# A gated delta-rule layer: the four steps of a block decayed at once, their carries by stored products, and a new order around them

## The reference

```python
def step(S, xs):
    q_t, k_t, v_t, a_t, b_t = xs
    Sk = jnp.einsum('bhvk,bhk->bhv', S, k_t)
    S = a_t[..., None] * S - (b_t[..., None] * (Sk - v_t))[..., None] * k_t[:, :, None, :]
    o_t = jnp.einsum('bhvk,bhk->bhv', S, q_t)
    return (S, o_t)
```

## Time and profile before

| | |
|---|---|
| median of 3 runs | 2696.94 us (2694.35 to 2698.34) |
| profiled execution | 2697.37 us, its span 2695.6 us |
| mean granted TensorE clock | 0.889 |
| busy | PE 2205.7 us, DVE 1928.7, ACT 1279.0, POOL 555.7 |
| transfers | 434.41 MB in 211139 packets |

### The profile page before, as it was taken

One profiled execution on the slowest core, in us unless ns is written; L12 is line 12 of the kernel. 1 busy time (PEld: TensorE's weight loads), 2 busy tenths in 40 slices (PEclk: granted clock), 3 DMA queues, 4 the chain that ended last, 5 costly groups with the idle time before them and its releaser, 6 DMA issues.

```text
span 2695.6 us, 61331 instructions
## 1 busy us (share of the span) xinstructions
PE 2205.7 (82%) x21482; PEld 1634.8 (61%) x21482; DVE 1928.7 (72%) x4376; ACT 1279.0 (47%) x2731; POOL 555.7 (21%) x580
## 2 busy tenths in 40 slices
PE   5999999999937778777877777787787773599998
PEld 3445888888736667666766666666676662244443
DVE  5222899999928878888887888888888788133334
ACT  2000787778715445444544544554454450334433
POOL 0000343444432212212222222122122222000000
PEclk9999999999958888788887888978888895799999
DMA  6000477667775455555555554554555554301210
GB/s 235 8 8 13 161 270 273 236 234 275 275 255 181 155 194 172 180 167 179 178 170 179 171 193 151 184 189 155 186 180 157 192 172 140 137 5 73 78 62 24
DMA packets 211139, 434.41 MB, mean 161 GB/s; under 512 B 47152, under 2 KB 160552, under 8 KB 181720
## 3 DMA queue, kind: packets, MB, share of 16 engines
q1 hardware_dynamic: 210856, 430.95, 46.8%
q0 software_dynamic: 48, 0.16, 0.0%
HBM read 295.13 MB, written 136.98 MB: 160 GB/s over the span
## 4 chain that ended last, share of the span: by engine, by line
PE 49%; DVE 23%; issue 13%; ACT 12%; DMA 1%; DVEq 1%; POOL 1%; ACTq 0%; SPq 0%; POOLq 0%
PE PS L1342 11%; DVE arena L945 8%; ACT arena L740 5%; PE PS L1454 4%; PE PS L1481 4%; PE PS L1330 4%; PE PS L1294 3%; PE PS L1244 3%; PE PS L1221 3%; DVE arena L972 2%; DVE arena L1000 2%; ACT arena L745 2%; PE PS L1467 2%; PE PS L1476 2%; PE PS L1356 2%
## 5 line engine op out<-in xcount | busy, mean ns | idle before, releaser
L1244 PE MATMUL PS<-arena 128*128 x2048 | 463.6, 387 | 1.8 <-DVEq L930 0.9
L945 DVE SCALAR_TENSOR_TENSOR arena<-PS,SM,arena 128x256 f32<-128x256 f32 x1152 | 452.8, 474 | 15.5 <-ACT arena L650 15.5
L1244 PEld LDWEIGHTS PS<-arena 128*128 128x128 f32 x2048 | 383.8, 188 | 81.6 <-DVE arena L945 6.5
L1342 PE MATMUL PS<-arena 128*128 128x128 f32 x1920 | 340.0, 331 | 84.5 <-ACT arena L745 84.5
L1342 PEld LDWEIGHTS PS<-arena 128*128 128x128 f32 x1920 | 286.9, 229 | 126.4 <-ACT arena L745 101.7
L577 POOL TENSOR_TENSOR arena<-arena 128x256 f32<-128x256 f32 x128 | 114.6, 896 | 1188.6 <-DVE arena L1044 1188.6
L740 ACT ACTIVATE arena<-arena 128x128 f32<-128x128 f32 x960 | 302.0, 394 | 32.9 <-DVE arena L989 32.3
L650 ACT ACTIVATE arena<-PS,SM 128x256 f32<-128x256 f32 x384 | 209.5, 564 | 89.3 <-PE PS L1244 84.3
L766 ACT COPY arena<-PS 128x512 f32<-128x512 f32 (+1 forms) x188 | 91.1, 521 | 304.6 <-PE PS L1369 304.2
L1330 PE MATMUL PS<-ident,arena 128*128 128x128 f32 x960 | 184.9, 326 | 61.0 <-ACT arena L740 60.2
L754 ACT COPY arena<-PS 128x256 f32<-128x256 f32 x240 | 89.5, 373 | 257.7 <-PE PS L1342 256.7
(11 more groups left out here) (134 smaller groups left out, 3558.2 us busy)
## 6 DMA issues: line engine op xcount, KB each, us to landing
arena<-g_d SPq DMA_DIRECT2D x128, 1024.0 KB, 5.1
arena<-vas_d SPq DMA_DIRECT2D x128, 384.0 KB, 3.2
vas_d<-arena SPq DMA_DIRECT2D x32, 1024.0 KB, 10.1
kq_d<-arena SPq DMA_DIRECT2D x8, 4096.0 KB, 11.5
arena<-kq_d SPq DMA_DIRECT2D x16, 2048.0 KB, 8.2
arena<-beta_d SPq DMA_DIRECT2D x8, 2048.0 KB, 9.1
kb_d<-arena SPq DMA_DIRECT2D x8, 2048.0 KB, 10.3
vas_d<-arena SPq DMA_DIRECT2D x8, 2048.0 KB, 12.5
```

Source lines behind the costliest of these rows:

```text
L945: nc.vector.scalar_tensor_tensor(acc, raw[:, :, i:i + PT_], CW[:, w, i, hh:hh + 1], acc, ALU.mult, ALU.add).then_inc(job_free if i == TAPS ...
L1244: ins = mm(dst.rearrange("p (b n) -> p b n", b=B), W4[:, w, kt, DH * h:DH * (h + 1)], XNT[:, kt, :, bass.ds(c * PT_ + (HALO - halo), halo ...
L1342: ins = mm(bank(7)[:, 128 * gi:128 * (gi + 1)].rearrange("v (l x) -> v l x", l=NB), STR[:, s % 2, gi, :], KQ[d][:, :, p0:p0 + 2].rearrange ...
```

## The change

Each block decays all its reads at once by products from the block's start (`dec`), adds all values at once (`add`), and decays a write to the later steps of the block (`carry`) before it is weighed. The products needed (1, a1, a1*a2, a2, a0, a0*a1, a0*a1*a2: `ND_` = 7 a step group) are made by GpSimd in the projection (`steps`, a quarter of the heads at a time, in a tile for one quarter), stored to `t_d` and loaded with GB. `NACC` falls from 6 to 3. In the order of the chunk loop: VectorE adds state slots right behind a block's copy for blocks 0 to 4; TensorE issues g4 ahead of g0 in blocks 1 and 3; ScalarE copies g0 there after its read copies. In `carry(1)` the factors 0:4:3 are 1 and a2.

```diff
-NACC = 6
+NACC = 3
+ND_ = 7
+    t_d = dram("t_d", (128, NS * NB, ND_ * NP))
+        TSTf = take(PSC * NB * ND_ * NP // 4)
+        DT = take(2 * ND_ * NP).rearrange("v (b p x) -> v b p x", b=2, x=ND_)
+        DW = take(3 * NP).rearrange("v (p x) -> v p x", x=3)
...
+                def store_steps(q):
+                    w = ND_ * NP // 4
+                    sp.wait_ge(t_step, c * 20 + 5 * q + 6)
+                    sp.dma_start(t_d[:, blocks, w * q:w * (q + 1)], TSTf.rearrange("v (l x) -> v l x", x=w)).then_inc(t_stored, 16)
+                store_steps(0)
                 store_decays(0)
                 sp.wait_ge(silu_done, c * NQ + NACC + 2 * NQ // 3)
                 sp.dma_start(kq_d[two].rearrange("s k x -> k s x"), ...).then_inc(kq_stored, 16)
+                store_steps(1)
                 sp.wait_ge(kb_step, c * 8 + 8)
                 sp.dma_start(kb_d[two].rearrange("s k x -> k s x"), ...).then_inc(kb_stored, 16)
                 store_suffixes(0)
+                store_steps(2)
                 store_decays(1)
+                store_steps(3)
...
+                sp.dma_start(DT[:, m % 2].rearrange("v p x -> v (p x)"), t_d[:, at(n * NB + m)].rearrange("v l x -> v (l x)")).then_inc(t_in[m % 2], 16)
...
+                def steps(q):
+                    a, k = AQ[:, q], c * 20 + 5 * q + 1
+                    pool.wait_ge(a_ready, c * 4 + q + 1)
+                    pool.wait_ge(t_stored, c * 64 + 16 * q + 64)
+                    if q == 0:
+                        pool.wait_ge(t_step, k)
+                    tt(TS[..., 5], a[..., 0], a[..., 1], ALU.mult).then_inc(t_step, 1)
+                    tt(TS[..., 2], a[..., 1], a[..., 2], ALU.mult).then_inc(t_step, 1)
+                    nc.gpsimd.tensor_copy(TS[..., 1:4:2], a[..., 1:3]).then_inc(t_step, 1)
+                    nc.gpsimd.tensor_copy(TS[..., 4], a[..., 0]).then_inc(t_step, 1)
+                    pool.wait_ge(t_step, k + 4)
+                    tt(TS[..., 6], TS[..., 5], a[..., 2], ALU.mult).then_inc(t_step, 1)
...
                         if x == NQ // 3:
+                            steps(0)
                             pool.wait_ge(beta_in, c * 16 + 16)
...
                     if x == 6:
+                        steps(1)
                         suffixes(0)
+                steps(2)
+                steps(3)
                 suffixes(1)
...
                         act.wait_ge(sf_stored[i // 4], c * 16 + 16)
+                        act.wait_ge(t_stored, c * 64 + 32 * (i // 4) + 32)
...
-                        if k > 0:
+                        if k > 0 and m not in (1, 3):
                             next_evac()
...
-                    def add(t):
-                        tt(W[:, :, t], V[:, :, t], W[:, :, t], ALU.add).then_inc(v_add, 1)
-                    def dec(t):
-                        xs = Xb[:, :, :, t + 1:4]
-                        tt(xs, xs, A[:, :, t].unsqueeze(2).unsqueeze(3).to_broadcast([128, NP, 2, 3 - t]), ALU.mult).then_inc(x_dec, 1)
+                    def dec():
+                        dve.wait_ge(corr_sub, n * N_SUB + (9 if m == 0 else SUB_AT[m - 1] + 1))
+                        dve.wait_ge(t_in[m % 2], n * 64 + (16 * (m // 2) + 16))
+                        xs = Xb[:, :, :, 1:4]
+                        tt(xs, xs, wide(D[:, :, 4:7], 0), ALU.mult).then_inc(x_dec, 1)
+                    def add():
+                        dve.wait_ge(x_dec, n * NB + m + 1)
+                        tt(W, V, W, ALU.add).then_inc(v_add, 1)
+                    def carry(t):
+                        ...
+                        tt(DW[:, :, t:3], W[:, :, t].unsqueeze(2).to_broadcast([128, NP, 3 - t]), f, ALU.mult).then_inc(w_dec, 1)
...
-                    dec(0)
+                    dec()
+                    add()
+                    carry(0)
                     weigh(0)
-                    add(1)
-                    sub(0)
...
+                    sub(0)
+                    carry(1)
                     weigh(1)
-                    dec(1)
-                    add(2)
-                    sub(1)
...
+                    sub(1)
                     weigh(2)
-                    dec(2)
-                    add(3)
...
-                    if m == 3 and nxt:
-                        state_add(6)
-                        state_add(7)
+                    if nxt and m < 5:
+                        state_add(2 * m if m < 4 else 10)
+                        state_add(2 * m + 1 if m < 4 else 11)
...
-                    if bk == 0:
+                    if bk == 0 or what == "g4":
                         pe.wait_ge(corr_sub, ...)
...
+                    if m == 1 or m == 3:
+                        preps.reverse()
```

More of the change, by code:

```diff
@@ L262, in build @@
         e_stored, half_bias = sem("e_stored"), sem("half_bias")
+        t_step, t_stored, t_in, w_dec = sem("t_step"), sem("t_stored"), [sem(f"t_in{i}") for i in range(2)], sem("w_dec")
         kq_in = [sem(f"kq_in{i}") for i in range(2)]
@@ L340, in _ @@
                 sp.sem_inc(stored, 16)
+            sp.sem_inc(t_stored, 64)
             sp.wait_ge(xnT_ready, 8)
@@ L419, in _ @@
                 sp.wait_ge(stored, 16 * NPC + 16)
+            sp.wait_ge(t_stored, 64 * NPC + 64)
             sp.wait_ge(job_full, NPC * NJ)
@@ L519, in _ @@
             ES = EST.rearrange("v (s r p) -> v s r p", s=PSC, r=7)
-            with pool.Fori(0, NPC) as c:
+            TS = TSTf.rearrange("v (l p x) -> v l p x", p=NP // 4, x=ND_)
+            AQ = ASTf.rearrange("v (l q p t) -> v q l p t", q=4, p=NP // 4, t=BL)
+            for stored in base_stored:
+                pool.wait_ge(stored, 16 * NX // 2 + 16)
+            pool.wait_ge(beta_stored, 16 * B)
+            nc.gpsimd.memset(TS[..., 0], 1.0).then_inc(t_step, 1)
+            with pool.Fori(0, NPC) as c:
+                def steps(q):
[10 more added lines that the diff above has]
+                    tt(TS[..., 6], TS[..., 5], a[..., 2], ALU.mult).then_inc(t_step, 1)
                 def suffixes(hf):
@@ L562, in _ @@
                 pool.wait_ge(stored, 16 * NPC + 16)
+            pool.wait_ge(t_stored, 64 * NPC + 64)
             for tile in (S, PT32, KBT):
@@ L696, in _ @@
                 act.wait_ge(stored, 16 * NPC + 16)
+            act.wait_ge(t_stored, 64 * NPC + 64)
             act.wait_ge(zeros, 5)
@@ L969, in head_sub @@
                     dve.wait_ge(corr_full, n * 9 + 1 + hf)
-                    if b == 0:
-                        dve.wait_ge(v_add, n * NB * BL + 1)
+                    if b == 0 and hf == 0:
+                        dve.wait_ge(x_read, 1 + n * 16)
                     tt(dst, dst, src, ALU.subtract).then_inc(corr_sub, 1)
@@ L980, in level_sub @@
                     dve.wait_ge(nested, n * 7 + NEST_BEFORE[m])
-                    if k == 0:
-                        dve.wait_ge(v_add, (n * NB + m + 1) * BL + 1)
                     tt(dst, dst, src, ALU.subtract).then_inc(corr_sub, 1)
@@ L1033, in weigh @@
                             dve.wait_ge(gb_in[m % 2], n * 64 + (16 * (m // 2) + 16))
-                            dve.wait_ge(v_add, k4 + 1)
-                        else:
-                            dve.wait_ge(x_sub, k3 + t)
-                        tt(TMP[:, :, 0:6 - 2 * t].rearrange("v p (e t) -> v p e t", e=2), GB[:, m % 2, :, t, :, t + 1:4],
-                           W[:, :, t].unsqueeze(2).unsqueeze(3).to_broadcast([128, NP, 2, 3 - t]), ALU.mult).then_inc(wg_mul, 1)
+                        if t < 2:
+                            dve.wait_ge(w_dec, (n * NB + m) * 2 + t + 1)
+                            w = DW[:, :, t:3]
+                        else:
+                            dve.wait_ge(x_sub, k3 + 2)
+                            w = W[:, :, 2:3]
+                        tt(TMP[:, :, 0:6 - 2 * t].rearrange("v p (e t) -> v p e t", e=2), GB[:, m % 2, :, t, :, t + 1:4], wide(w, t), ALU.mult).then_inc(wg_mul, 1)
                     def sub(t):
                         dve.wait_ge(wg_mul, k3 + t + 1)
-                        dve.wait_ge(v_add, k4 + t + 2)
                         xs = Xb[:, :, :, t + 1:4]
@@ L1046, in chunk @@
                     Pt, at = {4: (P4, 0), 8: (P8, 4), 16: (P16, 12), 32: (P32, 28)}[LEVEL[m]]
-                    add(0)
                     if m == 0:
@@ L1111, in chunk @@
                         for s in ADD_AT[m]:
-                            if m != 3 or s >= 8:
+                            if m >= 5 or m == 3 and s >= 8:
                                 state_add(s)
```

19 lines of the change are left out of this document (8 added, 11 removed).

## The result

The changed kernel takes 2681.6 us (median of 5 runs, 2679.7 to 2683.5), the kernel before, run beside it, 2694.6 (5 runs, 2694.1 to 2698.3). The ratio is 0.9948, interval [0.9934, 0.9963]: 14 us faster by the ratio, where 24 were forecast. The profiled execution has a span of 2681.2 us against 2695.6, 14.4 less. That difference is split here.

A forecast was written before the change was run, and what follows sets the result against it. It took VectorE to bound the projection and no engine alone the chunk loop. Loop -40, projection +7 and tail +9 gave -24 from 2697.4: 2673 us, own range 2655 to 2690, 80% range 2630 to 2715.

The forecast's parts named there:

- The chunk loop, -40: Chunk loop: 2.65 us off a chunk as a mean, fifteen times, with small terms for last and first chunk; net 40 us off.
- the mask wait: Block 1 to 2: VectorE's 3.53 us idle for the g4 mask moves to the corrections and is no gain of that size.
- TensorE's clock moves: Rival, chunk loop: granted clock rises from 0.83 to 0.86, 19 us more off, twice that at 0.89; chance 0.18 for up.
- Block 0 to 1: Chunk loop: ScalarE's and TensorE's waits go; 1.6 us off in one chunk of a pair, 0.5 in the other.
- Block 1 to 2: Chunk loop: TensorE's wait for ScalarE's scaling falls, 1.2 us off a chunk.
- The block arithmetic, 0.15 to 0.42 us a block: Chunk loop: VectorE 0.4 us less busy a block; 0.15 us counts from corrections to copy, 0.4 at block 3 to 4.
- The projection, +7: Projection: the suffix store lands 3 to 5 us later, VectorE stalls 1.0 us an iteration, seven times: 7 us.
- the tail, +9: End of the projection: the last e store, which GpSimd's memsets wait for, lands 9 us later (6 to 14).
- GpSimd and its stores take turns: Rival, projection: calls of 4.9 us or packets of 33 ns lengthen the round round one tile; 2703 us, chance 0.14.
- the beta load 9 us later: Projection: the beta load moves back about 9 us, costing GpSimd 6 us, taken up by the wait for the kq transfer.
- the upper bound 38: Projection: by bytes alone a 448-byte packet costs 38 ns, a store 4.9 us, transfers 61.5 us an iteration, over the period.
- a doubling, 52 ns: Rival, projection stores: each 448-byte packet handled as a read and a write, 6.7 us a store; 2755 us, chance 0.08.

The follow-up runs named there:

- e3: The changed kernel with the old order of the chunk loop (products, stores and loads stay); 2724.0 us, ratio 1.0109.
- e4: The changed kernel with step products made by GpSimd in the chunk loop, two blocks ahead, none made or stored in the projection, NACC 6; 2644.8 us, ratio 0.9814.
- e2: The kernel before with the state additions alone moved right behind the copy, g4 and g0 as before; 2644.7 us, ratio 0.9815.
- e7: The changed kernel with two quarter tiles in turn for the step products and NACC 2; 2663.4 us, ratio 0.9877.
- e6: The changed kernel without GpSimd's step products in the projection, a tile of ones stored four times an iteration instead; 2661.3 us, ratio 0.9871.
- e5: The changed kernel with step products made but not stored, the chunk loop loading other data in their place; 2646.6 us, ratio 0.9819.
- e8: The changed kernel with one tile for half the heads, stored twice an iteration in 896-byte packets, NACC 2; 2684.2 us, ratio 0.9960.
- e12: The kernel before with g4 alone issued ahead of g0 in blocks 1 and 3, additions where they were; 2695.4 us, ratio 1.0002.

## Why the prediction was right, and where it was not

The direction and the range were right, the size was 14 instead of 24. That it came so near has luck in it: the loop gave 8 us more than forecast and the projection cost 19 more (35 for 16), and the loop's gain came by another way than the sum has it.

**The chunk loop, -40: measured -47.7.** The waits that the prediction named went, the mask wait went over to the corrections as it said, and it put no gain there. The sum had 2.65 us off each chunk; what happened is that 13 of 14 chunks became shorter by one step of some 3.5 us (95.6 to 92.1). With the clock's part taken out by the rough estimate above, 40 us are left; that this is the term itself is chance. The clock rose too, as in the rival "TensorE's clock moves": from 0.83 to 0.85 in the window of the earlier trace rows (0.86 was priced). Half of its matmul time was taken to be on the chain; the estimate has 0.4.

**The split of the 40 was wrong.** "Block 0 to 1" was given 1.6 and 0.5 us, 16 us in fifteen chunks: alone it gave 40 (24 without the clock, by the estimate). "Block 1 to 2" was given 1.2 us, 18 us: it gave 6.5. So a wait that the trace names as the last need not be worth its length. The two lengths of a chunk say how this can be: the additions moved in block 0 bring 13 chunks down by a step, those in block 1 three. Why a step is as long as it is, and how much of it is waits and how much clock, stays open; no run held the clock still.

**The block arithmetic, 0.15 to 0.42 us a block.** The busy saving came: in e3 VectorE is busy for 1151.2 us between the first and last `carried` instead of 1202.6, over 120 blocks 0.43 us a block, where 0.4 was taken. (The forecast's 320 ns for 128 elements was too low: the 128-element decay took 384 ns in the kernel before, and the carries now take 364 and 360. Removed and added instructions are both dearer, and the difference of 0.8 us a block stays.) On the time it gave 0.3 us a chunk with the old order (e3, three chunks a step shorter and the first one longer) and nothing beside the new one (e4 against e2). All of the change's cost is for this.

**The projection, +7, and the tail, +9: measured +20 and +15.** This is the step that failed. The forecast let the suffix store land 3 to 5 us later and VectorE stall for 1.0 us an iteration; the period grew by 3.1 us. What it had as the rival "GpSimd and its stores take turns" is what happened (iteration near 62, tail 14, priced at +46 together, measured +35), but under neither of its conditions: calls took 3.9 us as forecast, and packets 30 ns, below 33. What makes the round long is GpSimd's wait for the landings of the steps' own stores (89.6 us in all, 2.8 in e7). It falls before `steps(2)` and `steps(3)`, and so puts off all that follows in the round: the second suffixes, e, the beta load, k*beta, and the suffix store that ScalarE waits for. GpSimd's wait for the beta load, 46.5 us, doesn't measure the loss: it is 98 us in e7, whose chunk loop starts 20 us earlier. The forecast saw the beta load 9 us later and took it that the wait for the kq transfer would cover this. e7 shows the turns, e6 what the bytes alone cost.

**The packets.** The changed kernel, e5 and e8 differ in their transfers by the stores of the step products (e5's loads read another place, with as many bytes), so the queue's line of each page gives their price (packets, MB, share of the 16 engines over the span; in this order):

```profile
q1 hardware_dynamic: 295336, 489.68, 54.6%
q1 hardware_dynamic: 229288, 460.32, 50.6%
q1 hardware_dynamic: 262312, 489.68, 53.6%
```

0.546 x 2681.2 - 0.506 x 2646.2 = 125 us for 32 stores, 3.9 us each and 125 x 16 / (295336 - 229288) = 30 ns a packet of 448 bytes. In e8 0.536 x 2678.2 - 0.506 x 2646.2 = 97 us for 16 stores, 47 ns a packet of 896 bytes. The forecast had 23 to 26 ns for 448 bytes and the upper bound 38, so its 12 to 13.5 us of transfer an iteration were 15.6. 448 bytes cost more than 512 bytes did in the earlier trace rows (26 ns), and per byte some 30% more than either of the larger packets; they do not cost two of them. The Trainium skill (DMA: Bandwidth & Descriptors, Specifications) says that transfers below 512 bytes lose line rate and become read-modify-writes. The loss of rate agrees, with these 30 against 26 ns; a doubling, 52 ns, is not what the runs show.

**What was costed at nothing and was nothing:** GpSimd's work beside the taps (e5: 2646.6 us, loop start as before), NACC = 3, the extra load a block, g4 ahead of g0 (e12).

**Where the best kernel lies.** The moved additions alone (e2, 2644.7 us) beat the changed kernel by 37 us and the kernel before by 50, with an edit of a few lines. The new blocks add nothing to it even when their products come almost free (e4).

## What to carry to other kernels

Before a helper result is stored in a stage whose transfers are already dense, count the turns round its staging tile and not only the bytes: two tiles took 20 of 35 us away here, where half as many packets, twice as large, took away two. When an edit joins an order change and an arithmetic change, run each alone; here one did all and the other paid all. And where no engine is the bound, a short instruction moved ahead of a waiting one (50 us here) can be worth far more than instructions saved on the busiest engine (5 us alone, nothing beside it). Before the gain of one place is read as so much a chunk, look at the length of each chunk: here they come in steps, and a mean hides them.

## What the runs showed of the hardware

- The chunks of this loop have two lengths, 91.4 to 93.0 us and 94.7 to 96.3, in 193 of 196 chunks of fourteen profiles, and none between.
- TensorE's granted clock moves with small shifts in the order of others' work: one pair of additions moved in one block raised it from 0.85 to 0.88 in the loop, and the same matmuls took 39 us less.
- Moving more additions (e2) took 23 us of idle time more from TensorE, and the clock fell back to 0.87, so that the matmuls took 17 us more again; the time still fell by 10 us.
- GpSimd's products of 256 elements took 0.67 to 0.68 us as a two-input product, and 205 us more of its busy time in the chunk loop (e4) left VectorE's weighings and subtractions as they were (558 and 556 ns for 384 elements); its decay and addition took slightly longer (570 for 555 ns, 443 for 426).
- A stored packet of 448 bytes took 30 ns of a transfer engine and one of 896 bytes 47 ns (the changed kernel and e8, each against e5).
- In the dense stage an issue of a transfer can hold SP's queue itself: 3.58 us at 518.61 where others take 0.37.
